# Edges of the second graph layer in compact lists of their own, split by halves of the column number

## What is computed

```
h = relu(layernorm(x))                                  # layer 1: graph attention, 4 heads of 32
wh = h @ weight ; e[i,j] = leaky_relu(src(wh[i]) + dst(wh[j]), 0.2)
x = x + softmax_j(where(adj[i,j] > 0, e, -9e15)) @ wh
h = relu(layernorm(x))                                  # layer 2: message passing into a GRU cell
msg = relu((adj @ h) @ W_msg.T + b_msg)
r, z = sigmoid(...), sigmoid(...) ; n = tanh(i_n + r * h_n)
x = x + (1 - z) * n + z * h
```

## Time and profile before

| what | value |
|---|---|
| median of 3 runs | 1139.23 us (1138.23 to 1144.86) |
| the profiled execution | 1144.6 us, its span 1142.9 us |
| TensorE matmul | busy 682.9 us, 60% |
| ScalarE | 661.7 us, 58% |
| GpSimd | 632.1 us, 55% |
| VectorE | 601.9 us, 53% |
| HBM | 298.83 MB read, 12.71 MB written |
| adjacency loads, last mask made | 763 us |
| layer 2's gathers | 854 to 1115 us |

### The profile page before, as it was taken

One profiled execution on the slowest core, in us unless ns is written; L12 is line 12 of the kernel. 1 busy time (PEld: TensorE's weight loads), 2 busy tenths in 40 slices (PEclk: granted clock), 3 DMA queues, 4 the chain that ended last, 5 costly groups with the idle time before them and its releaser, 6 DMA issues. The chain is left out here.

```text
span 1142.9 us, 12964 instructions
## 1 busy us (share of the span) xinstructions
PE 682.9 (60%) x3821; PEld 504.4 (44%) x3821; DVE 601.9 (53%) x2542; ACT 661.7 (58%) x664; POOL 632.1 (55%) x622
## 2 busy tenths in 40 slices
PE   1573752666666657666676676664231766766685
PEld 0452631544545545544454454543231544544453
DVE  7446542665674674674665656656230343344345
ACT  2574671987987978878878878862130222322232
POOL 5011155754654664664655664756507777777770
PEclk9787885887887887887888888885556788887878
DMA  9999696999999999999999999930102222222221
GB/s 318 358 417 353 227 414 240 368 413 415 401 416 413 407 416 413 407 413 398 406 407 403 408 403 386 405 110 22 24 13 53 49 65 59 68 65 67 57 65 41
DMA packets 59075, 308.09 MB, mean 270 GB/s; under 512 B 16385, under 2 KB 34003, under 8 KB 42624
## 3 DMA queue, kind: packets, MB, share of 16 engines
q1 hardware_dynamic: 27936, 274.74, 59.5%
q0 software_dynamic: 20480, 25.75, 8.7%
q10 hardware_dynamic: 10592, 6.82, 2.0%
HBM read 298.83 MB, written 12.71 MB: 273 GB/s over the span
## 5 line engine op out<-in xcount | busy, mean ns | idle before, releaser
L467 ACT ACTIVATE ind<-adj_in 128x4144 bf16<-128x4144 int32 (+1 forms) x128 | 462.4, 3613 | 65.0 <-DMA adj_in<-in_adj 61.1
L602 PE MATMUL ps<-ind,bit_w 128*128 128x296 bf16 (+1 forms) x1792 | 318.1, 337 | 48.0 <-ACT ind L467 47.8
L412 POOL DMA_INDIRECT rows_in<-wh_table,idx x192 | 203.2, 1058 | 216.6 <-issue 197.3
L602 PEld LDWEIGHTS ps<-ind,bit_w 128*128 128x128 bf16 x1792 | 199.6, 114 | 146.4 <-ACT ind L467 64.9
L1085 POOL DMA_INDIRECT adj_in<-g_table,nbr_idx x192 | 202.5, 1055 | 90.7 <-issue 58.2
L417 POOL DMA_INDIRECT vals_in<-in_adj,val_idx x192 | 199.7, 1040 | 58.5 <-issue 58.5
L1218 DVE TENSOR_TENSOR adj_in<-adj_in,nbr_val 128x1536 f32<-128x1536 f32 x16 | 28.1, 1759 | 166.0 <-DMA adj_in<-g_table,nbr_idx 166.0
L1415 PE MATMUL ps<-ident,adj_in 128*128 128x128 f32 x128 | 41.4, 424 | 95.2 <-DVE adj_in L1218 95.2
L841 DVE MAX8 cand<-ps 128x8 f32<-128x148 f32 x256 | 62.0, 305 | 53.6 <-PE ps L602 52.9
L1415 PEld LDWEIGHTS ps<-ident,adj_in 128*128 128x128 f32 x128 | 32.7, 314 | 99.2 <-DVE adj_in L1218 99.2
L425 POOL DMA_DIRECT2D wh_table<-t_buf x16 | 12.1, 759 | 114.9 <-DVE t_buf L795 114.9
(11 more groups left out here) (234 smaller groups left out, 1386.1 us busy)
## 6 DMA issues: line engine op xcount, KB each, us to landing
adj_in<-in_adj SPq DMA_DIRECT2D x64, 2072.0 KB, 17.5
adj_in<-in_adj SPq DMA_DIRECT2D x64, 2024.0 KB, 17.8
wh_table<-t_buf POOLq DMA_DIRECT2D x16, 264.0 KB, 8.3
g_table<-t_buf ACTq DMA_DIRECT2D x16, 256.0 KB, 24.1
out<-ind SPq DMA_DIRECT2D x16, 256.0 KB, 2.3
rows_in<-wh_table,idx POOLq DMA_INDIRECT x192
vals_in<-in_adj,val_idx POOLq DMA_INDIRECT x192
adj_in<-g_table,nbr_idx POOLq DMA_INDIRECT x192, 2.8
```

The lines of the kernel that those rows point to most:

```text
L412: nc.gpsimd.indirect_dma_start(out=rows_in[:, par, t, k, :], out_offset=None, in_=wh_table, in_offset=bass.IndirectOffsetOnAxis(ap=idx[:, ...
L467: nc.scalar.activation(ind[:, t % 2, a:b], adj_in[:, slot, 0:b - a].bitcast(I32), ACT.Relu, bias=1.0, scale=-1.0, accum_out=empty[:, bass. ...
L602: ins = nc.tensor.matmul(o[:, 0:w], bit_w[:, b, :], ind[:, t % 2, c0:c0 + w], start=False, stop=(b == BITS - 1))
```

## The change

- **Own lists for layer 2.** For each group of four tiles and for each half of the column number (below 4096, from 4096 on) there are now five places of 128 edges: one per tile and one that the four tiles share for what does not fit. So a group has ten places (E2 = 10) instead of twelve. They are built by new steps in the scan: `count2`, `offsets2`, `differences2`, `edges2` on VectorE, `places2`, `neighbours2`, `send_lists2` on TensorE.
- **Values.** GpSimd gathers the ten values of each layer-2 place; layer 1 no longer gathers values and takes each listed edge for an edge. A check at the end compares.
- **Low half early.** In the drain GpSimd gathers the five low places of every group (`early_rows`) from the first half of `g_table`; TensorE sums them (`early`), ScalarE stores the sums with the bias (`early_out`). In the second block only the five high places are gathered (`late_rows`); VectorE adds the early sum (`add_early`).
- **Weights inside the masks.** The value is multiplied into the 0/1 mask (`own2`, a ring of four), not into the gathered rows. The mask of the shared place is 512 wide.
- **Buffers.** Six table buffers in the place of `rows_in`, six gather buffers; the bias rows move to the general path; the loops of the second block are written out.

The core of the diff:

```diff
-                            nc.gpsimd.indirect_dma_start(
-                                out=vals_in[:, par, t, k:k + 1], out_offset=None, in_=adj_values,
...
+                def values(s):
+                    pool.wait_ge(idx2_done, s + 1)
+                    for k in range(E2):
+                        nc.gpsimd.indirect_dma_start(
+                            out=val2[:, s, k:k + 1], out_offset=None, in_=adj_values,
...
+                def early_rows(q):
+                    if q >= RING2:
+                        pool.wait_ge(early_mm, q - RING2 + 1)
+                    for k in range(5):
+                        nc.gpsimd.indirect_dma_start(
+                            out=edges_in[:, q % RING2, k, :], out_offset=None, in_=g_table[0:HN, :],
...
+                rows(0)
+                for s in range(1, NG - 1):
+                    rows(s)
+                    values(s - 1)
                 for par in range(2):
+                    pool.wait_ge(g_out[par], 16 * (NG // 4))
+                pool.wait_ge(ind_done, 2 * T - 3)
+                for q in range(LEAD):
+                    early_rows(q)
+                rows(NG - 1)
+                values(NG - 2)
+                for q in range(LEAD, NG - 2):
+                    early_rows(q)
+                values(NG - 1)
+                for q in range(NG - 2, NG):
+                    early_rows(q)
```

`send_lists2` is 16 small fp32 matmuls, `places2` and `neighbours2` two each; `offsets2` waits for `places2`, `differences2` for `neighbours2`, `edges2` for `send_lists2`, and TensorE waits once for the first `differences2` (`after_done`) before it projects the last group. Most of `differences2` are two compares of 8 x 128 elements:

```diff
+                    for h in range(2):
+                        ins = V.tensor_tensor(after_off[:, h], iota[:].unsqueeze(1).to_broadcast([P, 2 * G, P]),
+                                              off2[:, h].rearrange("p k g -> p (k g)").unsqueeze(2).to_broadcast([P, 2 * G, P]), ALU.is_ge)
+                    ins.then_inc(after_done, 1)
...
                     if m == 9:
-                        bias_rows()
+                        bias_sums()
...
-                    if q >= 2:
-                        dve.wait_ge(table_out[q % 2], (q // 2) * 16)
+                    if q >= TBUFS:
+                        dve.wait_ge(table_out[q % TBUFS], (q // TBUFS) * 16)
```

The second block (the first new `body` is VectorE's, the second TensorE's, which had `aggregate2(q + 1)`; a sum is now one 512-wide and four 128-wide fp32 matmuls, was twelve 128-wide):

```diff
+                    def late_rows(q):
+                        e = NG + q
+                        if q >= RING2:
+                            pool.wait_ge(agg2_mm, q - RING2 + 1)
+                        for k in range(5):
...
-                        V.tensor_tensor(r, r, nbr_val[:, tiles(q * G), :].rearrange("p g k -> p (g k)").unsqueeze(2)
-                                        .to_broadcast([P, 3 * G, D]), ALU.mult).then_inc(weighted2, 1)
+                    def prepare(q):
+                        if q >= OWNS:
+                            dve.wait_ge(agg2_mm, q - OWNS + 1)
+                        w = own2[:, q % OWNS]
                         for t in range(G):
+                            V.tensor_scalar(w[:, t, :], iota1[:, t * P:(t + 1) * P], edge_row2[:, q, t:t + 1], val2[:, q, t:t + 1], ALU.is_equal, ALU.mult)
+                        V.tensor_scalar(w[:, G:2 * G, :].rearrange("p k r -> p (k r)"), iota1[:], edge_row2[:, q, G:G + 1], val2[:, q, G:G + 1],
+                                        ALU.is_equal, ALU.mult).then_inc(own2_done, 1)
+                    def add_early(q, k):
+                        dve.wait_ge(agg2_mm, q + 1)
+                        V.tensor_tensor(early_sum[:, q, :], ps[:, 6 + k % 2, :], early_sum[:, q, :], ALU.add).then_inc(sum_done, 1)
...
+                    def body(q, k):
+                        if q + 2 < NG:
+                            prepare(q + 2)
+                        candidate(q)
+                        if q >= 1:
+                            add_rows(q - 1, (k - 1) % RING)
+                        if q + 2 < NG:
+                            add_early(q + 2, (k + 2) % RING)
+                        mix(q, k)
...
                     def aggregate2(q, k):
-                        pe.wait_ge(weighted2, q + 1)
+                        e = NG + q
+                        if q >= 2:
+                            pe.wait_ge(sum_done, q - 1)
+                        pe.wait_ge(own2_done, e + 1)
+                        pe.wait_ge(edges_landed[e % RING2], 16 * 5 * (e // RING2 + 1))
+                        nc.tensor.matmul(o, r[:, G, :], w[:, G:2 * G, :].rearrange("p k r -> p (k r)"), start=True, stop=False)
                         for t in range(G):
+                            ins = nc.tensor.matmul(o[:, t * P:(t + 1) * P], r[:, t, :], w[:, t, :], start=False, stop=(t == G - 1))
...
+                    def body(q, k):
+                        if q + 1 < NG:
+                            turn2(q + 1, (k + 1) % RING)
+                        if q + 2 < NG:
+                            aggregate2(q + 2, (k + 2) % RING)
+                        gates(q, k)
+                        if q >= 1:
+                            rows_back(q - 1, (k - 1) % RING)
```

More of the change, by code:

```diff
@@ L44 @@
 A_DMAS = 2 * H
-B_DMAS = 9 + 7
+B_DMAS = 7
 XC = 16
+HN = N // 2
+E2 = 10
+C2 = K + 5
+TBUFS = 6
+RING2 = 6
+OWNS = 4
+LEAD = 6
 RING = 4
@@ L276, in gat_gru_kernel @@
         gathered = [sem(f"gathered{i}") for i in range(2)]
+        counted2 = sem("counted2")
+        off2_mm = sem("off2_mm")
+        send2_done = sem("send2_done")
+        shift_mm = sem("shift_mm")
+        after_done = sem("after_done")
+        list2_mm = sem("list2_mm")
+        list2_read = sem("list2_read")
+        idx2_done = sem("idx2_done")
+        values_in = [sem(f"values_in{i}") for i in range(2)]
+        own2_done = sem("own2_done")
+        early_mm = sem("early_mm")
+        early_done = sem("early_done")
+        gen_bias_clear = sem("gen_bias_clear")
+        gen_bias_in = sem("gen_bias_in")
+        gen_bias_done = sem("gen_bias_done")
         crest_done = sem("crest_done")
@@ L423, in store @@
[L423 to L437 removed]
+                            ).then_inc(gathered[s % 2], 16)
@@ L549, in body @@
                         exps(s - 2)
+                    if s == NG:
+                        for q in range(4):
+                            early_out(q)
+                    if s == NG + 1:
+                        early_out(6)
+                        early_out(7)
                 schedule(act, body)
+                for q in range(8, NG):
+                    early_out(q)
             @block.tensor
@@ new lines, in send_lists2 @@
+                def send_lists2(s):
+                    pe.wait_ge(after_done, s + 1)
+                    if s >= 1:
+                        pe.wait_ge(list2_read, s)
+                        pe.wait_ge(var2_done, s)
+                    else:
+                        pe.wait_ge(whbar_done, 1)
+                    for h in range(2):
+                        for t in range(G):
+                            nc.tensor.matmul(ps_list2[:, h * 5 + t, :], after_off[:, h, t, :], dsend[:, t, :], start=True, stop=True)
+                        for t in range(G):
+                            ins = nc.tensor.matmul(ps_list2[:, h * 5 + G, :], after_off[:, h, G + t, :],
+                                                   dsend_over[:, t - 1, :] if t else dsend[:, 0, :], start=(t == 0), stop=(t == G - 1))
+                    ins.then_inc(list2_mm, 1)
@@ new lines, in early @@
+                def early(q):
+                    if q >= 2:
+                        pe.wait_ge(early_done, q - 1)
+                    pe.wait_ge(own2_done, q + 1)
+                    pe.wait_ge(edges_landed[q % RING2], 16 * 5 * (q // RING2 + 1))
+                    r, w = edges_in[:, q % RING2], own2[:, q % OWNS]
+                    nc.tensor.matmul(ps[:, q % 2, :], r[:, G, :], w[:, G:2 * G, :].rearrange("p k r -> p (k r)"), start=True, stop=False)
+                    for t in range(G):
+                        ins = nc.tensor.matmul(ps[:, q % 2, t * P:(t + 1) * P], r[:, t, :], w[:, t, :], start=False, stop=(t == G - 1))
+                    ins.then_inc(early_mm, 1)
@@ L667, in body @@
                         aggregate(s - 3, 1 - par)
+                    if s == NG + 1:
+                        early(4)
+                        early(5)
                     if "c" in do:
                         pack(s, 0)
+                    if "b" in do:
+                        send_lists2(s - 2)
                     if "t" in do:
@@ L1337, in _ @@
                     messages(0, 0)
-                    for q in range(RING):
-                        body(q, q, q > 0)
-                    with act.Fori(1, NG // RING - 1) as i:
-                        for k in range(RING):
-                            body(i * RING + k, k)
-                    for k in range(RING):
-                        q = NG - RING + k
-                        body(q, k, True, NG - 1 - q)
+                    for q in range(NG):
+                        body(q, q % RING, q > 0, NG - 1 - q)
             @block.tensor
@@ L1455, in _ @@
                     aggregate2(0, 0)
-                    for q in range(RING):
-                        body(q, q, q > 0)
-                    with pe.Fori(1, NG // RING - 1) as i:
```

(8 more changed lines are left out.)

391 lines of the change are left out of this document (254 added, 137 removed).

## The result

The changed kernel takes **1173.73 us** (median of 4 runs, 1170.51 to 1178.76) beside 1142.05 for the kernel before on the same chip (1138.23 to 1150.59): ratio 1.027, 95% interval 1.020 to 1.034. 1177 was predicted, slower with a chance of 0.75. As a difference, +38 us was predicted and +31.7 came between the medians. The execution in the profile took 1170.51 us, its span is 1168.0, against 1142.9 before: 25.1 us more.

What follows compares the result with a forecast made beforehand. DMA queues were taken to bound the scan, GpSimd's issuing the drain and layer 2. Start -19, scan 0, drain +84, layer 2 -27 sum to +38 on 1142.9: span 1181, median 1177 us; own range 1155 to 1197, 8 in 10 1138 to 1199.

Steps and rivals of the forecast that it cites:

- Start: Before the scan: bias rows and table waits go, fewer gathers precede the first child logits; gain 19 us, bounds 6 and 25.6.
- VectorE's first gather wait near 10 us: Sign for the start: VectorE's first wait for gathers would be near 10 us.
- Scan: Bodies 3 to 15: added VectorE and TensorE work costs nothing, hidden under the DMA queues; period still 43.5 us.
- the scan is no longer hidden: Rival, scan: VectorE's and TensorE's chain passes 43.5 us per group, 1.5 us x 13 = 20 us, total 1197; chance 0.13.
- Drain: From `rows(14)` to layer 2: 134 gathers in GpSimd's queue at 1.33 us each; 84 us lost, bounds 77 and 93.
- Layer 2: Second block: gates, candidate, tanh, mix, mask and sum run serially, 16.2 us per round; 27 us gained, bounds 63 and 15.
- The masks don't hold up the sums: Rival, layer 2: it runs at TensorE's pace, 8.4 us per group, 128 us gained, total 1076 us; chance 0.10.
- TensorE keeps its upper clock: Rival, layer 2: round of 14.0 us, total 1148 us, or below 1139 with quick masks and full start; chance 0.14.
- 1155 to 1197: Whole kernel: the forecast's own range in us, from its bounds; 1138 to 1199 was given to hold 8 in 10.
- The masks' price: Layer 2, VectorE: four 128-wide masks at 0.3 us each, overlapped, and 0.7 for the 512-wide one; 1.9 us together.

Runs made afterwards that it cites:

- the exchange of the two steps: Changed kernel with VectorE's `row_maximum(s-2)` put ahead of `offsets2(s-1)` in the scan: 1164.84 us, ratio 1.015.
- a wait of 13.5 us put into the queue: Changed kernel with all low-half gathers issued after `rows(15)` and `values(14)` in GpSimd's drain queue: 1187.32 us, ratio 1.035.
- kernel with masks earlier: Changed kernel with layer 2's mask of group q+3, not q+2, made ahead of the candidate of group q: 1074.63 us, ratio 0.938.
- the first two experiments: Changed kernel with layer-2 masks one group earlier: 1074.63 us; changed kernel with TensorE's sum of group q+2 behind the gates of group q: 1064.53 us.
- the three kernels without the stand of 5 us: Changed kernel with masks one group earlier, 1074.63 us; sum behind gates, 1064.53 us; both plus offsets behind the row maximum, 1055.06 us.

## Why the prediction was right

**Start** (predicted -19, bounds 6 and 25.6): -35.2 us at group 3, outside the bounds. The bound was worked out from the idle time of the DMA queues from 100 to 202 us. The part before 100 us was not looked at: there group 1 is already 10.6 us ahead. Within the part looked at, the prediction counted 7 for bias rows and table waits together, less the added steps; bias rows gave 4.0 and the table buffers 16.9. Of the 8.4 us that it read as bias rows, 2.7 are the clearing of a buffer, which goes with the table buffers. Fewer gathers ahead of the first child logits gave 8.8 where 11.5 was counted. "VectorE's first gather wait near 10 us" measured 12.9.

**Scan** (predicted 0, "hidden under the DMA queues"): this step failed. Groups take 44.3 us, not 43.5; from group 3 to the last mask 11.2 us of the start's gain are given back (35.2 at group 3, 24.0 at the last mask). That the two errors cancel to 5 us is luck. The rival "the scan is no longer hidden" named the mechanism (`offsets2` waits for TensorE and delays the maxima), and the exchange of the two steps confirmed it for about half; its price was 20 us and came to 11. What misled was counting VectorE's idle time, 17 us per group. ScalarE is busy for only 35.5 of 44.3 us, but its steps in between come late by 0.2 to 3.6 us, 8.7 in all, and so it has no slack. Which part of the added work makes the rest of these waits was not separated.

**Drain** (+84, bounds 77 and 93): +81.8. The terms: (901.43 - 726.11) / 133 = 1.32 us per gather against 1.33 taken; 9.2 us from the last low-half gather to the first of layer 2 against 10.3. Undoing 64 of the 134 gathers took 61 us back, and a wait of 13.5 us put into the queue came out at the end of the drain as 15.3. The mechanism is shown.

**Layer 2** (-27, bounds 63 and 15): -31.3; 257.4 us against 261.6. The 13 rounds average 15.8 us where 16.2 was taken, and that makes the difference but for half a us. The round of 16.1 us that is shown above, by its terms, predicted and measured: gates to the end of the mix with `add_early` 10.5 and 10.9 (6.15 to the candidate, 4.71 to the first mask); masks 1.9 and 1.7; sum 1.8 and lower clock 2.2 on both sum and gates, together 4.0, and 3.5 for the sum, with 0.7 more inside the 10.9, in the first gate. The clock's part by itself: in the kernel with masks earlier the 512-wide pass takes 653 ns where after takes 1086, and the whole difference of the four groups of matmuls, (31.5 - 18.2) + (29.1 - 19.3) + (23.5 - 17.2) + (17.8 - 16.3) = 30.9 us over 14 rounds, is 2.2 us each. These are their rows in that kernel, sum and first two gates:

```profile
L1655 PE MATMUL ps<-adj_in 128*128 128x128 f32 x128 | 19.3, 301 | 0.0
L1653 PE MATMUL ps<-adj_in 128*128 128x512 f32 x32 | 18.2, 653 | 11.9 <-DMA adj_in<-g_table,idx 11.9
...
L1664 PE MATMUL ps<-ind,wT 128*128 128x512 f32 x32 | 17.2, 622 | 0.0
L1666 PE MATMUL ps<-ind,wT 128*128 128x512 f32 x32 | 16.3, 592 | 0.0
```

and in the kernel after:

```profile
L1652 PE MATMUL ps<-adj_in 128*128 128x512 f32 x32 | 31.5, 1086 | 79.5 <-issue 67.8 <-DMA adj_in<-g_table,idx 11.7
...
L1654 PE MATMUL ps<-adj_in 128*128 128x128 f32 x128 | 29.1, 405 | 0.0
...
L1663 PE MATMUL ps<-ind,wT 128*128 128x512 f32 x32 | 23.5, 829 | 0.0
...
L1665 PE MATMUL ps<-ind,wT 128*128 128x512 f32 x32 | 17.8, 638 | 0.0
```

**The rivals.** "The masks don't hold up the sums" (1076 us, 8.4 us per round) did not happen, but is just what the first two experiments made: 1074.6 and 1064.5. "TensorE keeps its upper clock" did not happen: from 950 to 1030 us its clock reads 0.82 in the kernel after, and 1.00 in the three kernels without the stand of 5 us.

**The total.** The parts were wrong by 6.4 us at the last cut ahead of the drain, 2.2 in the drain and 4.3 in layer 2, all to the slow side: 12.9 us between the two traces, and 6 between the medians (+38 against +31.7). That 1177 lies only 3 us from 1173.73 owes the other 3 to the kernel before, which measured 1142.05 here and 1139.23 when the prediction was made. The range "1155 to 1197" is not the same at both ends: its upper end is the root of the summed squares of the bounds, and taken that way the lower end is 1140.

**The masks' price.** The wide mask takes 0.54 us, between the 0.7 taken and the 0.43 of the 512-wide copy. From a 128-wide mask (341 ns) to a 512-wide one (541 ns) 384 elements more cost 200 ns, 0.52 ns each, where the 1024-wide tensor-tensor compare (1217 ns) costs 525 ns more than the 512-wide one, 1.03 ns each. The Trainium skill (VectorE: DVE Perf Modes, the perf-mode tier table) has fp32 tensor_scalar from SBUF at twice the elements per cycle of fp32 tensor_tensor; on the slope the trace agrees, two column operands or not, while the fixed part of this form is some 115 ns more than the copy's.

## What to carry to other kernels

When a change takes away what bounds a stage, write down the loop that is left, in the order of both queues: here masks made one step later than needed cost 99 us, where they last 1.7 us in each of 14 groups, and exchanging two calls on TensorE gave 109 back. A stage whose DMA queues read 0.98 busy need not be bound by them: ask whether anyone still waits for the data (ScalarE, before 5.5 us per group, after none). And bound a gain over the whole stretch it can reach, not from the first window in which it was noticed.

## What the runs showed of the hardware that was not expected

A second chip ran every kernel slower, the one before by 18% (1345.52 against about 1143 us), with instructions of the same length: the mask of ScalarE takes 3.61 us on both. What differs are stalls on several engines, most of them 3 to 14 us long, from 158 us on, for which the trace names no work of the program. In the trace of the kernel before without bias rows:

```profile
PEld ps L598 <- issue: 217.2, 178, 9.2
...
DVE zsafe L947 <- remote: 131.0, 14, 14.4
```

Their cause is open.

A gather of layer 2 on GpSimd takes 0.94 to 0.95 us by itself and 1.2 us beside masks on VectorE. In the kernel with the masks earlier, GpSimd,

```profile
963.64 1.22 POOL L1308 DMA_INDIRECT adj_in<-g_table,idx  x1 [0.30 <-issue]
965.16 1.18 POOL L1308 DMA_INDIRECT adj_in<-g_table,idx  x1 [0.30 <-issue]
966.64 0.95 POOL L1308 DMA_INDIRECT adj_in<-g_table,idx  x1 [0.30 <-issue]
```

and VectorE:

```profile
963.96 1.11 DVE L1452 TENSOR_SCALAR adj_in<-iota,edge_row,val 128x128 f32<-128x128 f32 x4
964.98 0.54 DVE L1453 TENSOR_SCALAR adj_in<-iota,edge_row,val 128x512 f32<-128x512 f32 x1
```

The same pair comes in each of its settled rounds. So a mask costs GpSimd about 0.5 us per group, which is nothing while TensorE sets the round. The Trainium skill (SBUF — State Buffer, "Who interferes with whom") has tensor_scalar in its two-port modes and GpSimd shut each other out of a port pair, descriptor writing for GpSimd's own DMAs included. The rows agree in that masks and gathers meet. They don't show a stand for the whole 1.65 us of the masks: each gather loses some 0.25 us, less than one mask's length (0.34 us, the wide one 0.54). Nor are masks the only instructions that do this. Beside the first two instructions of the mix, tensor-tensor with both inputs in SBUF (L1478 and L1481), the gathers of the same trace take 1.09 to 1.41 us, while beside those that read one input from PSUM (L1463, L1466, L1473, L1458) they stay at 0.94 to 0.95. In which part of a gather the neighbour must fall is not shown; a few that touch a mask stay at 0.94 too.
